# An attention and mixture-of-experts layer: another pace for GpSimd's indirect transfers, 18 batches in the first group instead of 20, and 15 batches summed last instead of 13

## What is computed

```python
x = layernorm(x + attn(x))     # xa = x @ Wm_attn.T, batch norm over all tokens, q, k, v;
                               # causal softmax(q k^T / sqrt(128)) v, then two projections
x = layernorm(x + ffn(x))      # router: softmax over 8 experts, the top 2 per token
# expert(x) = gelu(_ln(x) @ W1.T + B1) @ W2.T + B2;  out = sum over the two experts of gate * expert
```

## Time and profile before

| | |
|---|---|
| time, median of 3 runs | 557.65 us (557.21 to 558.38) |
| the profiled execution's own time | 552.77 us |
| its span, from the first to the last instruction | 550.7 us |
| mean granted TensorE clock | 0.930 of full speed |
| PE busy, ACT, POOL, DVE | 456.7, 331.9, 281.1, 266.4 us |

### The profile page before, as it was taken

The page is one execution under the profiler, slowest core; times in us unless marked ns, Lnnn a source line. Parts: engine busy times, 40 slices in busy tenths (PEclk is TensorE's granted clock), DMA queues, the critical chain, the costliest instruction groups (busy, mean ns, idle before and its releaser), DMA issues.

```text
span 550.7 us, 14356 instructions
## 1 busy us (share of the span) xinstructions
PE 456.7 (83%) x3465; PEld 417.0 (76%) x3465; DVE 266.4 (48%) x1544; ACT 331.9 (60%) x876; POOL 281.1 (51%) x335
## 2 busy tenths in 40 slices
PE   8987677788897247888778888887999999999984
PEld 8876455677786237788777778776999999999964
DVE  1466344457786154332122455422333378878624
ACT  3066254467675227555455655655778888999817
POOL 4005255566566722455546555555445556666732
PEclk9999798789899557889989999999999999999997
DMA  9992011111111111222222222222222345555365
GB/s 250 366 403 69 26 39 41 40 40 50 41 45 47 49 35 38 70 64 59 73 78 76 69 64 70 64 64 58 71 70 70 108 135 166 166 164 172 104 205 183
DMA packets 59951, 55.12 MB, mean 100 GB/s; under 512 B 8243, under 2 KB 52147, under 8 KB 59875
## 3 DMA queue, kind: packets, MB, share of 16 engines
q1 hardware_dynamic: 51088, 35.91, 22.8%
q0 software_dynamic: 8416, 17.51, 9.6%
q10 hardware_dynamic: 370, 0.80, 0.5%
HBM read 31.42 MB, written 22.77 MB: 98 GB/s over the span
## 4 chain that ended last, share of the span: by engine, by line
PE 73%; another core or an unknown queue 8%; ACT 8%; issue 6%; DMA 2%; DVE 1%; ACTq 1%; SPq 0%; POOL 0%; DVEq 0%; POOLq 0%
PE bank L908 23%; PE bank L918 23%; PE bank L901 4%; PE bank L773 3%; ACT xT L1084 3%; PE bank L719 2%; PE bank L759 2%; PE bank L803 2%; PE bank L794 2%; PE bank L782 1%; PE bank L949 1%; PE bank L805 1%; PE bank L804 1%; PE bank L784 1%
## 5 line engine op out<-in xcount | busy, mean ns | idle before, releaser
L621 POOL DMA_INDIRECT queue<-x_all,pos_i x128 | 123.1, 962 | 125.1 <-PE bank L918 39.7
L639 POOL DMA_INDIRECT ybuf<-xT,yrow x135 | 131.3, 972 | 104.8 <-DVE yrow L1540 41.5
L918 PE MATMUL bank<-w2T,xT 128*128 x1080 | 148.0, 281 | 26.8 <-ACT xT L1084 25.2
L918 PEld LDWEIGHTS bank<-w2T,xT 128*128 128x128 f32 x1080 | 133.7, 195 | 32.1 <-issue 32.0
L908 PE MATMUL bank<-xT 128*128 128x128 f32 x1080 | 149.4, 283 | 3.0 <-ACT xT L964 3.0
L908 PEld LDWEIGHTS bank<-xT 128*128 128x128 f32 x1080 | 134.8, 196 | 3.6 <-ACT xT L964 3.5
L964 ACT ACTIVATE xT<-w1T,zero_col 128x512 f32 x135 | 97.2, 721 | 27.4 <-issue 22.3
L1530 DVE TENSOR_TENSOR xT<-bank,b_bc 128x128 f32<-128x128 f32 x135 | 39.4, 292 | 152.3 <-PE bank L918 117.3
L1084 ACT ACTIVATE xT<-bank 128x512 f32<-128x512 f32 x135 | 78.6, 582 | 44.8 <-PE bank L908 39.2
L964 ACT ACTIVATE xT<-bank,one_col 128x128 f32<-128x128 f32 x135 | 49.0, 363 | 23.8 <-PE bank L901 20.3
L1537 DVE TENSOR_SCALAR xT<-xT 128x128 f32<-128x128 f32 x135 | 46.3, 343 | 8.8 <-issue 4.2
(11 more groups left out here) (251 smaller groups left out, 721.2 us busy)
## 6 DMA issues: line engine op xcount, KB each, us to landing
xT<-queue SPq DMA_DIRECT2D x135, 66.0 KB
w1r<-ybuf SPq DMA_DIRECT2D x24, 256.0 KB, 5.6
x_all<-x SPq DMA_DIRECT2D x16, 256.0 KB, 6.2
xT<-x_t SPq DMA_DIRECT2D x8, 512.0 KB, 9.6
out<-x_all SPq DMA_DIRECT2D x32, 128.0 KB
ybuf<-xT,yrow POOLq DMA_INDIRECT x135
w1r<-w_t SPq DMA_DIRECT2D x8, 256.0 KB, 5.5
w2T<-w_t SPq DMA_DIRECT2D x8, 256.0 KB, 11.1
```

Source lines behind the costliest of these rows:

```text
L621: pool.indirect_dma_start(out=queue, out_offset=bass.IndirectOffsetOnAxis(pos_i[:, b, t, c:c + 1], 0), in_=x_all[:, b * TPB + t, DATA:DATA ...
L639: pool.indirect_dma_start(out=ybuf, out_offset=bass.IndirectOffsetOnAxis(yrow[:, j % IR:j % IR + 1], 0), in_=ysb[:, q, :], in_offset=None) ...
L918: last = mm(bank[4 + s][:, 0:P], hs[:, s, h, :], w2T[:, bass.ds(e, 1), h, :].rearrange("p a d -> p (a d)"), start=(h == 0), stop=(h == HC ...
```

## The change

**The first group** is made of 18 batches instead of 20 (`NB0`), so it has 65 tiles and is counted two steps earlier; the second has 70.

**The pace.** Every single indirect transfer of POOL now has a count to wait for, not every second one. Its number n in POOL's own order counts scatters and results together. The 72 of the first group wait for `s_y` (PE's steps): four steps for eleven transfers up to n = 27, four steps for nine after that. All others wait for `s_yy` (PE's tiles), `(n - 72) * 2 // 3 - 5`, until the result sent is the one that the rule names; that is at tile 97.

**The order on POOL.** The scatters of batches 18 to 24 come in a row, then three results come between the scatters of each later batch. The rows below are POOL's program as it stands in before: after the constants come 84 scatters, one iota, 44 scatters, and then results only.

```diff
-    NB0 = 20
+    NB0 = 18
     NTILE0 = 2 * NB0 * TPB - (E - 1)
...
-        FIN = 19
+        FIN = 17
...
-        UNITS = [(FIN,)] + [(n, n + 1) for n in range(FIN + 1, NB - 2, 2)] + [(NB - 2,), (NB - 1,)]
+        UNITS = [(FIN,)] + [(n, n + 1) for n in range(FIN + 1, NB, 2)]
...
-            def after_pe(b, t):
-                n = TPB * b + t
-                if b < NB0:
-                    wait(pool, s_y, min(NB, 2 + n // 2 if n < 16 else 11 + (n - 16) * 25 // 32))
-                else:
-                    wait(pool, s_yy, (n - TPB * NB0 - 6) * 4 // 3)
...
+            FIRST_SENT = 2 * TPB * NB0
+
+            def after_steps(n):
+                wait(pool, s_y, 2 + n * 4 // 11 if n < 28 else min(NB, 12 + (n - 28) * 4 // 9))
+
+            def after_tiles(n, j):
+                tiles = (n - FIRST_SENT) * 2 // 3 - 5
+                if j < tiles:
+                    assert tiles < j + YR - 1
+                    wait(pool, s_yy, tiles)
+
+            def scatter(b, n, j):
                 pool.wait_ge(s_pos, b + 1)
                 own_wait(pool, s_own_pool)
                 for t in range(TPB):
-                    after_pe(b, t)
                     for c in range(2):
+                        if n + 2 * t + c < FIRST_SENT:
+                            after_steps(n + 2 * t + c)
+                        else:
+                            after_tiles(n + 2 * t + c, j)
                         pool.indirect_dma_start(
...
-            for b in range(NB):
-                scatter(b)
-                if b == NB0:
-                    second_pads()
-
-            def result_step(j, q, use, known):
-                if j < 60:
-
-                    ahead = 23 + 2 * j // 3
-                    assert j < ahead < j + YR
-                    pool.wait_ge(s_yy, ahead)
+            def result_step(j, q, n):
+                after_tiles(n, j)
                 wait(pool, s_ys, j + 1)
...
+            IN_A_ROW, BETWEEN = 6, 3
+            sent, j = 0, 0
+            for b in range(NB):
+                scatter(b, sent, j)
+                sent += 2 * TPB
+                if b == NB0:
+                    second_pads()
+                if b >= NB0 + IN_A_ROW:
+                    for j in range(j, j + BETWEEN):
+                        result_step(j, j % YR, sent)
+                        sent += 1
+                    j += 1
...
                 if has[-1]:
                     make_z(ahead)
-                    start_v(ahead)
-                    start_scores(ahead)
-                if k - 3 in EARLY:
-                    rank(k - 3)
                 if has[4] and k - 4 > EARLY[-1]:
                     rank(k - 4)
                 if has[-1]:
-                    make_v(ahead)
+                    start_v(ahead)
+                    start_scores(ahead)
                 if has[1]:
                     turn_p(k - 1)
+                if k - 3 in EARLY:
+                    rank(k - 3)
                 if has[-1]:
+                    make_v(ahead)
                     scores(ahead, ahead % 2)
...
                 if has[-1]:
                     copy_z(k + 1)
-                    copy_v(k + 1)
                 if has[1]:
                     copy_p(k - 1)
+                if has[-1]:
+                    copy_v(k + 1)
```

21 lines of the change are left out of this document (13 added, 8 removed).

## The result

The changed kernel takes 536.9 us (533.95 to 537.28, four runs) against 557.4 us for the kernel before, timed beside it: a ratio of 0.963, with a 95% interval of 0.9585 to 0.967. That is 20.5 us less, where -7 was forecast. The mechanism was the one named, but the gain is three times as large.

What follows compares the result with a forecast made beforehand. PE was taken to bound the kernel, its signals held while POOL issues indirect transfers back to back. Terms -14 - 6 - 9 + 20 + 2 = -7 us gave 557.65 - 7 = 550.65 us, range 536 to 567.

Steps and rivals of the forecast that it cites:

- six steps: Attention steps from 59.7 to 99.3 us: half lose one transfer and PE's clock rises; -6 us, bounds 0 and -12.
- 17 steps: Attention steps from 99.3 to 173 us: nine transfers in four steps shorten them; -14 us, bounds -8 and -16.
- passage: Attention to tiles, 173 to 207.1 us: ten transfers after a later wait, 25 us against 34.1; -9 us, bounds -4 and -15.
- order of the step: Reordering inside the attention step: PE is busy for all of a clean step, so worth 0.
- tiles: Tile stages: transfers shed by attention prolong the paced stretch to tile 97 at 2.60 us each; +20 us, bounds +15 and +25.
- end: Last units on ACT: two ones become twos and the last store doubles; +2 us, bounds +1 and +4.
- the 2 for fours: Until tile 45: extra cost partly from runs of four would be +7 us; a third taken, as the rule cuts them.
- The ring of results: Tiles: results waiting between scatters have a ring of 32; result 21 goes at tile 45, needed free at 53: no new wait.
- rival B: Tiles: waiting for each transfer breaks runs into twos, 2.05 us a tile, about 500 us in all; chance 0.04.
- Rival C: Whole kernel: the pace isn't what holds PE, so only the end moves, +2 us, 559 us; chance 0.06.
- Rival D: Attention gives more than taken, all at its bounds: -43 + 20 + 2 = -21, 537 us; chance 0.20.
- The estimate of +1.2: End: two more loads of 256 KB, at 2.0 us a transfer plus bytes at 436 GB/s, estimated to add +1.2 us.

Runs made afterwards that it cites:

- chip B: Second chip of the experiments; the unedited changed kernel, run there again, took 542.7 us against 558.5 for before, ratio 0.969.
- old order: Changed kernel with the attention step of PE and ACT back in its earlier order (rank, products for v and turn_p as before): 538.4 us, ratio 0.963.
- second comparison: Changed kernel without an edit, timed again beside the kernel before: 542.7 us against 558.5, ratio 0.969.
- chip C: Third chip of the experiments, where PE's signals aren't held; unedited changed kernel 454.9 us against 446.5 for before, ratio 1.019.
- gap: Changed kernel with two small memsets on POOL behind each transfer of the tiles up to result 80, 0.75 us between transfers: 540.5 us, ratio 0.965.

## Why the forecast had the direction and not the size

By the table of stretches, term by term, with the first profile of the changed kernel and with the second (chip B), both against the one profile of before:

| term | forecast | first | second | |
|---|---|---|---|---|
| start | 0 | -3.1 | -2.3 | profiles of one kernel differ by as much |
| six steps | -6 | -8.2 | -6.7 | right |
| 17 steps | -14 | -12.6 | -10.3 | right: steps of 3.1 and 4.5 us, as the earlier trace rows and the pair of tiles said |
| passage | -9 | -9.2 | -8.3 | right |
| order of the step | 0 | 0 | | right in the time (old order: same ratio) |
| tiles | +20 | +11.3 | +16.6 | **failed**: mis-sized |
| end | +2 | +3.3 | +3.3 | within its bounds, in part by luck |
| sum | -7 | -18.5 | -7.7 | spans: -18.6 and -7.8; timed: -20.5 and -15.8 |

The mechanism was right. PE was held by back-to-back transfers, the attention gave what fewer transfers there were said to give, and the tiles took part of it back. The step that failed is the size of the tiles' term, +20 us at 2.60 us a tile, of which +11.3 came in the first comparison: 8.7 of the 13.5 us between forecast and result. Of the rest 3.1 us are in the start, 2.2 in the six steps, and 1.9 come from the profiled executions, which lie 4.9 us (before) and 2.9 us (after) below their medians; the 17 steps and the end lie 1.4 and 1.3 us the other way. In the second comparison the tiles' term is inside its bounds (+15 to +25). The spans differ by only 7.8 us there and the medians by 15.8, since the one profile of before (552.8 us) lies 4.9 us below its median and the second profile of the changed kernel (544.8 us) 2.1 us above its own.

Where the tiles' term was off can be said in part. The working stands under *The tiles*: "Within a pair of tiles the rule is as before (two behind one tile, one behind the next), so I see no reason for shorter runs than three." The rate is as before, but the count to wait for now stands ahead of each transfer and not of each second scatter, and until tile 45 most of what POOL sends is scatters. There 8 transfers go in single file and only 2 runs of four come about, where before had none and 5. The first 48 tiles took 118.7 us; the prediction's working gives them 48 x 2.60 plus the 2 for fours, 126.8. But the kernel with the old order of the step has exactly the same counts of runs and took 123.2, and the one with pairs, with 7 runs of four, took 124.2. So half of these 8 us is no more than how profiles differ, and that shorter runs make the other half is argued, not shown. From tile 48 on, where results go in threes as assumed, the forecast was 83.2 for 32 tiles and 82.7 came. From tile 80 to 134 it was 121.4 and 120.9 came, but that agreement is luck: the 9.6 us in which POOL catches up didn't come at tile 97, and a wait of SP that the working didn't have ("so no new wait") came at tile 86. The ring of results had been looked at, and not the wait for them in SP's program. The working also says that 182 transfers go at 1.5 a tile until tile 97; by the rule it is 145 (97 x 1.5), and the sum, made from 97 tiles, doesn't hang on it.

Waiting for each transfer was rival B's mechanism, given a chance of 0.04 and priced at its extreme (only runs of two, about 500 us). On chip B single waits for the scatters alone gave 0.981, the change with pairs instead of single waits 1.000, and the change 0.969 (0.963 in the first comparison). So single waits help, and without them the change gives nothing in the time. But they are not all of the gain, and by the stages not the larger part: with pairs the six steps, the 17 steps and the passage still give 22.7 us, by sending less there, and the tiles then cost 29.7 us more than before (340.7 against 311.0) instead of 11.3 to 16.6. What the pairs lose they lose mostly in tiles 48 to 96, with results, which went singly in the kernel before. That the length of runs is what the waits act through is shown for results between tiles 48 and 80 (a tile of 5.0 us beside a run of four, 3.2 beside a run of three; 91.7 us against 82.7 and 83.8), and for the other stages it is argued: 46 transfers in the 17 steps cost 73.6 us with five runs of four and 72.4 with none.

Rival C, that pace isn't what holds PE, is refuted where PE is held (gap, pairs), and on chip C the pace holds nothing. The rule behind it (the Trainium skill, "Advanced Engine Details and Errata", section "DMA Bandwidth Details": an increment of a semaphore costs about one cycle on trn2) doesn't conflict with chip C's 3.6 us for 135 gelus, but by itself it doesn't account for the 47.5 us of the other profile. Rival D's size (-21) came out by another sum: the attention gave 30 us (8.2 + 12.6 + 9.2), 29 of them forecast, not 43. The sharing-out of batches (18 and 15) is worth nothing or is a loss: 20 batches gave about the same ratio, and with the old end on top the ratio was the lowest.

The end grew by 3.3 us. With 20 batches and the new units it is 34.5, with the old units 32.9, with 18 batches 35.7: about half goes with the units, and what the rest is, is open. On the kernel before, the new units alone gave 32.6 against 32.4, so the term's own reason (two ones become twos, +1.5) doesn't show where it stands alone. The split rests on single profiles. The estimate of +1.2 that stands beside this term rests on a section of the Trainium skill ("DMA: Bandwidth & Descriptors", "Anatomy of one DMA") that is written for transfers which GpSimd issues; these loads of results, 256 KB each, are SP's, and in both profiles such a load lands 5.6 us after its issue (median).

Open: why chips differ (nothing in the rows of POOL or of its transfers does), why a run holds signals at all, the shortest gap that suffices between 0.30 and 0.75 us, since the kernels meant for it ran where nothing is held, and what the changed kernel would take on chip C with SP's later wait alone.

## What to carry to other kernels

Look for an engine's results that arrive in bunches after another engine's run of transfers, with a releaser that is long done or unnamed; then count how many transfers stand beside each stage and how long their runs are, and put the wait ahead of every transfer instead of every second. When work is moved later, list every wait in every queue that counts this work, SP's included, and not only the buffers that hold it. And before a pace is tuned, time the two kernels on more than one chip: this one is worth -3.1 to -3.7% on some and +1.9% on another.

## What the chip showed that was not expected

- While POOL issued indirect transfers of 0.96 us with 0.30 us between them, what PE had finished late in the run reached ACT only 0.76 to 1.08 us after the end of the last; with 0.75 us between them it came in time (2.05 us a tile). What PE finished between the first and the second transfer still passed at once (370.37 to 370.48).
- One chip did none of this with the same instructions: before takes 446.5 us there and 558.5 to 560.4 us on the two others, by far more than any edit here is worth. In the changed kernel the attention steps take 3.1 us each there (52.2 / 17) and the tiles 2.0 (95.7 / 48), and PE is busy for 60.80 of 60.80 us between tiles 48 and 80.
- Where PE is held, the price mostly moves with the transfers: more of them in the steps, another rate, or a gap beside the tiles changed which stretch pays, and the time stayed between 537.5 and 542.7 us. It is not one fixed price a transfer, though: from the eighth copy of z to tile 80 the changed kernel sends 186 transfers with single waits and with pairs alike, and takes 319 us with the one (329 in the second profile) and 341 with the other.
